# A decoder layer on one core: one cross attention unit's softmax by head on ScalarE, and the values of both segments in one product

## The reference

```python
def attn(x):            # self attention in segments
    qkv = x @ W_qkv     # 16 heads of 16
    q, k, v = ... [:, :, m]            # m: rows of 16 tokens, every second reversed
    # 2 segments of 128 queries; keys and values: every second token (64)
    p = softmax(q_seg @ k_seg.T * 16 ** -0.5)
    return (p @ v_seg)[inverse m] @ W_out

def xattn(x, ctx):      # cross attention, 16 heads of 16, 77 keys
    p = softmax((x @ Wq.T + bq) @ (ctx @ Wk.T + bk).T / 4)
    return (p @ (ctx @ Wv.T + bv)) @ Wo.T + bo

def ffn(x):             # 14 experts of width 512, one for each token
    e = argmax(x @ router_w); w = softmax(x @ router_w)[e]
    return w * (gelu(x @ w1[e] + b1[e]) @ w2[e] + b2[e])

x = layernorm(x + attn(x))
x = layernorm(x + xattn(x, ctx))
x = layernorm(x + ffn(x))
```

## Time and profile before

| | |
|---|---|
| median of 3 runs | 597.56 us (596.89 to 598.15) |
| the profiled execution's own time | 593.98 us |
| its span, first to last instruction | 592.2 us |
| PE, DVE, POOL, ACT busy | 560.5, 463.3, 405.7, 343.1 us |
| mean granted clock of TensorE | 0.977 of full speed |

### The profile page before, as it was taken

How to read it: one execution, slowest core, us unless ns; L and a number is a source line. 1 busy time by engine, 2 the same in 40 slices (tenths; PEclk the granted TensorE clock), 3 DMA queues, 4 the chain that set the end, 5 groups by cost and what they waited for, 6 DMA issues and landing times.

```text
span 592.2 us, 16640 instructions
## 1 busy us (share of the span) xinstructions
PE 560.5 (95%) x5608; PEld 474.9 (80%) x5608; DVE 463.3 (78%) x1071; ACT 343.1 (58%) x842; POOL 405.7 (69%) x554
## 2 busy tenths in 40 slices
PE   7989999999999999999999999799799999999990
PEld 5867788788888888788788778568789999999990
DVE  3778999999999999999999989865455555666661
ACT  2456666666666676676666765546545555555540
POOL 4446675678678677678678766675787677777652
PEclk9899999999999999999999999969989999999996
DMA  7416026126225314313514101114343333333200
GB/s 216 162 24 191 14 52 196 27 68 183 42 60 160 65 40 137 103 51 88 153 34 144 52 10 37 34 39 119 53 112 97 85 87 87 95 92 89 68 16 0
DMA packets 76692, 50.11 MB, mean 85 GB/s; under 512 B 39222, under 2 KB 70970, under 8 KB 76608
## 3 DMA queue, kind: packets, MB, share of 16 engines
q1 hardware_dynamic: 71264, 40.60, 25.5%
q0 software_dynamic: 5344, 8.44, 5.5%
HBM read 40.55 MB, written 10.60 MB: 86 GB/s over the span
## 4 chain that ended last, share of the span: by engine, by line
PE 74%; POOL 9%; issue 7%; DVE 5%; ACT 2%; DMA 1%; POOLq 0%; ACTq 0%; DVEq 0%
PE ps_r L822 15%; PE ps_r L740 13%; PE ps_s L956 11%; PE ps_r L972 10%; PE ps_r L807 5%; PE ps_r L902 5%; PE ps_s L762 4%; PE ps_s L753 3%; POOL token_lists L1579 3%; POOL prob L1498 2%; PE ps_r L795 2%; PE ps_r L879 2%; PE ps_r L897 2%; PE ps_r L904 2%; POOL out L1605 1%
## 5 line engine op out<-in xcount | busy, mean ns | idle before, releaser
L1498 POOL TENSOR_TENSOR prob<-prob,rden 128x616 f32<-128x616 f32 (+1 forms) x96 | 138.4, 1449 | 56.8 <-DVE rden L1173 55.1
L999 ACT COPY probT<-ps_r 128x512 f32<-128x512 f32 x192 | 86.8, 480 | 43.2 <-PE ps_r L740 41.4
L1141 DVE TENSOR_REDUCE mx<-ps_s 128x8 f32<-128x616 f32 (+1 forms) x96 | 88.8, 925 | 19.1 <-PE ps_s L753 12.8
L1019 ACT ACTIVATE prob<-prob 128x616 f32<-128x616 f32 (+1 forms) x96 | 79.4, 833 | 33.8 <-DVE prob L1152 33.6
L1161 DVE TENSOR_REDUCE den<-prob 128x8 f32<-128x616 f32 (+1 forms) x96 | 88.3, 920 | 6.9 <-ACT prob L1019 5.7
L1152 DVE TENSOR_TENSOR prob<-ps_s,mx 128x616 f32<-128x616 f32 (+1 forms) x96 | 89.8, 936 | 4.5 <-PE ps_r L740 3.0
L956 PEld LDWEIGHTS ps_s<-xgT,w1b 128*128 128x128 f32 x720 | 88.0, 193 | 2.5 <-issue 0.3
L740 PE MATMUL ps_r<-ident,prob 128*128 128x128 f32 (+1 forms) x576 | 88.4, 281 | 1.6 <-POOL prob L1498 1.0
L956 PE MATMUL ps_s<-xgT,w1b 128*128 128x128 f32 x720 | 88.6, 276 | 0.2 <-ACT xgT L1107 0.2
L972 PE MATMUL ps_r<-w2s,hT 128*128 x360 | 86.2, 383 | 0.3 <-ACT hT L1119 0.3
L740 PEld LDWEIGHTS ps_r<-ident,prob 128*128 128x128 f32 (+1 forms) x576 | 66.1, 142 | 16.8 <-issue 9.6
(11 more groups left out here) (158 smaller groups left out, 1006.1 us busy)
## 6 DMA issues: line engine op xcount, KB each, us to landing
w1s<-in_w SPq DMA_DIRECT2D x14, 512.0 KB
w2s<-in_w SPq DMA_DIRECT2D x14, 512.0 KB
b2r<-in_b SPq DMA_DIRECT2D x45, 128.0 KB, 3.2
xT<-in_x_cols SPq DMA_DIRECT2D x16, 256.0 KB, 2.9
xres<-in_x SPq DMA_DIRECT2D x16, 256.0 KB
x_rows<-x2s SPq DMA_DIRECT2D x32, 128.0 KB, 1.9
xkT<-in_xk_cols SPq DMA_DIRECT2D x16, 128.0 KB, 2.3
ctxT<-in_ctx_cols SPq DMA_DIRECT2D x16, 77.0 KB, 2.1
```

Source lines behind the costliest of these rows:

```text
L999: nc.scalar.copy(probT[0:rows, par, first:last], src[0:rows, 0:last - first]).then_inc(pT_copied[kind].sem, 1)
L1019: nc.scalar.activation(prob[:, n % 3, 0:width], prob[:, n % 3, 0:width], ACT.Exp, scale=SCALE).then_inc(exp_done[kind].sem, 1)
L1141: nc.vector.tensor_reduce(m, s, axis=AX, op=ALU.max).then_inc(max_done[kind].sem, 1)
L1498: nc.gpsimd.tensor_tensor(p, p, rden[:, par, 0:heads, None].to_broadcast([P, heads, width]), ALU.mult).then_inc(scaled[kind].sem, 1)
```

## The change

1. **Unit 5's softmax (`FUSED = ("x", 3)`).** DVE still takes the maxima, but then makes only `nmx`, the maxima times minus the scale (128x8). ACT reads the scores of each of the eight heads from `ps_s`, with `nmx` as bias, writes the exponentials to `prob` and sums them into `den` with `accum_out`: eight instructions in place of one. DVE's subtraction and its sum are gone for this unit, and the reciprocal waits for ACT.
2. **Who frees `ps_s` behind unit 5.** The next scores wait for `exp_done` (ACT), and so do the first two hidden layers of the expert tiles, which use the same banks.
3. **Values.** `v` is two matmuls of 128x256, keys of both segments on the partitions; ACT places them with four copies of 64x128 (segment by even or odd heads), half of which move them to the other 64 partitions.
4. **Order.** All tables are new, and so is `HELD`.

```diff
+        FUSED = ("x", 3)
+        def wait_read(eng, event, held="", part=""):
+            if event is not None:
+                done = exp_done if event[:2] == FUSED else sub_done
+                wait(eng, done[event[0]], event[2], event[1], held, part)
...
         def pe_scores(pe, n, i):
-            wait_for(pe, sub_done, unit_before(n, i, 1), held="pe_scores.1", part=n)
+            wait_read(pe, unit_before(n, i, 1), held="pe_scores.1", part=n)
...
             elif job == "v":
-                for s in range(NSEG):
-                    for c in range(KC):
-                        heads = wqkv_s[:, c, 2 * D:3 * D].rearrange("p (g o d) -> p g o d", o=2, d=DH)
-                        for o in range(2):
-                            last = nc.tensor.matmul(dst[o * KEYS:(o + 1) * KEYS, s * P:(s + 1) * P],
-                                                    xkT[:, b % 2, c, s, :], heads[:, :, o, :],
-                                                    start=(c == 0), stop=(c == KC - 1))
+                last = project(lambda c: xkT[:, b % 2, c].rearrange("p s k -> p (s k)"), lambda c: wqkv_s[:, c, 2 * D:3 * D])
...
         def pe_hidden(pe, j):
-                wait(pe, sub_done["x"], B - 1)
+                wait(pe, exp_done["x"], B - 1)
...
         def act_exp(act, n, i):
             wait(act, sub_done[kind], b, k, held="act_exp.1", part=n)
+            if (kind, k) == FUSED:
+                third = unit_before(n, i, 3)
+                if third is not None:
+                    wait(act, pT_done[third[0]], third[2], 2 * third[1] + 1, held="act_exp.2", part=n)
+                wait_for(act, rec_done, unit_before(n, i, 2), held="act_exp.3", part=n)
+                for h in range(HH):
+                    last = nc.scalar.activation(prob[:, n % 3, h * K2:(h + 1) * K2],
+                                                ps_s[:, h // RH, h % RH * K2:(h % RH + 1) * K2], ACT.Exp,
+                                                bias=nmx[:, h:h + 1], scale=SCALE, accum_out=den[:, par, h:h + 1])
+                last.then_inc(exp_done[kind].sem, 1)
+                return
...
             elif job == "v":
                 for o in range(2):
-                    rows = slice(o * KEYS, (o + 1) * KEYS)
-                    last = nc.scalar.copy(dst[rows, :, :, o, :],
-                                          src[rows, 0:2 * P].rearrange("p (s g d) -> p s g d", s=NSEG, d=DH))
+                    for n in range(NSEG):
+                        last = nc.scalar.copy(dst[o * KEYS:(o + 1) * KEYS, n, :, o, :],
+                                              from_ps[n * KEYS:(n + 1) * KEYS, :, o, :])
...
         def dve_less_max(dve, n, i):
             wait(dve, max_done[kind], b, k, held="dve_less_max.1", part=n)
+            if (kind, k) == FUSED:
+                wait(dve, exp_done[kind], b - 1, k, held="dve_less_max.3", part=n)
+                nc.vector.tensor_scalar(nmx[:], mx[:, par, 0:HH], -SCALE, None, ALU.mult).then_inc(sub_done[kind].sem, 1)
+                return
...
-        PE_TILES = "y@2 hid@0 rows@-1"
+        PE_TILES = "hid@-2 rows@-3 y@-1"
```

More of the change, by code:

```diff
@@ L38 @@
[L38 to L42, removed]
@@ L46 @@
+    "w1_copy.1:0",
 }
@@ L273, in decoder_layer @@
         exp_done = {u: signal(f"exp_done_{u}", n) for u, n in UN.items()}
-        sum_done = {u: signal(f"sum_done_{u}", n) for u, n in UN.items()}
+        sum_done = {u: signal(f"sum_done_{u}", n if u == "a" else n - 1) for u, n in UN.items()}
         rec_done = {u: signal(f"rec_done_{u}", n) for u, n in UN.items()}
@@ L379, in decoder_layer @@
-            probT50:15 probT51:15 wa:1 rows:0 gate_exp0:13 rt1:14 take_o4:15 take_o5:15 rows:1 gelu:0 rt0:15
-            gelu:1 rt1:15 rows:2 rows:3 wa:2 wa:3 gelu:2 gate_exp0:15 wa:4
+            qx0:13 take_o5:12 gate_exp0:11 probT00:14 probT01:14 take_o0:14 exp2:13 probT10:14 probT11:14
+            exp3:13 k0:15 exp4:13 take_o1:14 q0:15 probT20:13 probT21:13 exp5:13 vx0:14 probT30:13 probT31:13
+            rt0:12 take_o2:13 take_o3:13 probT40:13 kx0:14 probT41:13 probT50:13 x1T0:14 probT51:13 exp0:15
@@ L381, in decoder_layer @@
+            rt0:14 wa:0 take_o5:15 rows:0 rt1:14 wa:1 rows:1 gelu:0 gelu:1 rt0:15 rt1:15 rows:2 rows:3 wa:2 wa:3
+            gate_exp0:15 gelu:2 wa:4
         """
         DVE_FIRST = """
-            max0:0 wr0:0 less_max0:0 wr1:0 max1:0 less_max1:0 sum0:0 reciprocal0:0 sum1:0 reciprocal1:0 max0:1
-            wr2:0 less_max0:1 bo0:0 sum0:1 reciprocal0:1 max1:1 oa0:0 stats10:0 oa1:0 mean10:0 stats11:0
-            mean11:0 ln10:0 ln11:0 less_max1:1 sum1:1 reciprocal1:1 max2:0 less_max2:0 max3:0 less_max3:0 oa0:1
@@ L455, in decoder_layer @@
-            bias_row:1 store_x0:14 bias_row:2 slots:6 slots:7 bias_row:3 bias_row:4 store_x1:14 store_x0:15
-            store_x1:15 slots:8 slots:9 bias_row:5 slots:10
-        """
-        PE_TILES = "y@2 hid@0 rows@-1"
-        ACT_TILES = "wa@-2 rows@-2 gelu@-1"
-        DVE_TILES = "eps@1 bias@0 wd@-4 res@0 stat@0 norm@1 agg@0"
-        POOL_TILES = "gather@-3 pow@3 put@4"
-        SP_TILES = "slots@-2 bias_row@-2"
+            load_xres0:12 place_v0:11 load_e0:13 place_v1:11 place_v2:11 place_v3:11 place_v4:11 load_x0:15
@@ L463, in decoder_layer @@
+            bias_row:1 bias_row:2 bias_row:3 store_x1:13 store_x0:14 store_x1:14 bias_row:4 bias_row:5 slots:7
+            store_x0:15 store_x1:15 slots:8 slots:9 slots:10
+        """
+        PE_TILES = "hid@-2 rows@-3 y@-1"
+        ACT_TILES = "wa@1 gelu@2 rows@0"
+        DVE_TILES = "agg@3 eps@3 bias@2 res@2 wd@-3 stat@2 norm@3"
+        POOL_TILES = "gather@-4 pow@2 put@3"
+        SP_TILES = "slots@3 bias_row@4"
+        FUSED = ("x", 3)
         UNITS = [("a", 0), ("a", 1), ("x", 0), ("x", 1), ("x", 2), ("x", 3)]
@@ L1169, in dve_reciprocal @@
             heads = H if kind == "a" else HH
-            wait(dve, sum_done[kind], b, k, held="dve_reciprocal.1", part=n)
+            if (kind, k) == FUSED:
+                wait(dve, exp_done[kind], b, k, held="dve_reciprocal.1", part=n)
+            else:
+                wait(dve, sum_done[kind], b, k, held="dve_reciprocal.1", part=n)
             wait_for(dve, scaled, unit_before(n, i, 2), held="dve_reciprocal.2", part=n)
```

209 lines of the change are left out of this document (107 added, 102 removed).

## The result

The changed kernel takes 619.14 us (median; three of its runs lie between 617.85 and 619.83, the fourth was disturbed and is not in the ratio) against 597.53 us for the kernel before: ratio 1.0352, 95% interval [1.0316, 1.0388]. Forecast were 611.0 us, range 595 to 624. The profiled execution took 617.85 us, its span is 616.1 us. The experiments ran on four chips. On two of them the kernel before takes 595 to 596 us; on the other two it takes 635 to 638 us at a mean granted clock of TensorE of 0.93 to 0.95 (0.97 to 0.98 on the first two). So total times are compared by ratio on one chip, and pairs of batches in stretches at the upper level of the clock (2.4 GHz).

A forecast was written before the change was run, and what follows sets the result against it. The prediction took TensorE as the bound, full in the attention part. New waits +17.5 us, value product -2.6 and VectorE relief -1.5 gave +13.4: 607.4 us for the profiled execution, 611.0 us as the median, range 595 to 624.

The forecast's parts named there:

- TensorE's new wait at unit 0's scores, on ScalarE's last head: Between batches, scores wait until ScalarE has read unit 5's PSUM banks: 1.8 us in even batches, 0.9 in odd.
- E: Length of unit 5's eight ScalarE activations with sums: taken as 2.63 us, between 1.86 and 5.2 us.
- The fourth rival: Unit 5's activations: each sum costs an instruction of its own, E = 3.9 us, total 628 us; chance 0.08.
- The pair of batches: Steady attention part: a pair of batches takes 48.8 us instead of 46.4.
- The value product: Value projection on TensorE: 0.87 us instead of 1.03, saving 0.16 us 16 times, 2.6 us in all.
- The four copies at nothing: ScalarE's copies of the values: 0.34 us more per batch, costed at nothing since values are used half a batch later.
- VectorE, 22.6 us less: Unit 5's subtraction becomes a small product and its sum goes: 1.41 us less VectorE work per batch.
- half of TensorE's waiting near 380 us: Two score jobs there wait 2.98 us for VectorE; its relief was taken to save 1.5 us, ends 0 and 3.0.
- The order at nothing, 2 us either way: Start of the program: two batches' keys and queries projected before the first scores, some weights fetched later; costed at nothing.
- The second rival: Whole kernel: VectorE sets the pace, ScalarE has room and the activations overlap (E = 1.86), 594.3 us, faster; chance 0.20.
- The third: TensorE's clock: the new idle time in even batches sends it to its lower level, 15.6 us more, 626.6 us; chance 0.07.
- The fifth: The new waits fall where TensorE would have waited anyhow: -2.6 to 0 us, total 595 to 598 us; chance 0.05.

The follow-up runs named there:

- e3: Kernel before with only unit 5's eight activations added, old order and old value product kept: ratio 1.0129 to the kernel before.
- e6: Changed kernel with unit 5's eight activations handing over no sums (its divisions use unit 3's): 611.71 us against 596.45 for the kernel before.
- e12: The changed kernel itself, run again on another chip: ratio 1.0382 to the kernel before.
- e1: Kernel before with only the value product changed (one product for both segments, four ScalarE copies instead of two): 638.86 us against 638.37, ratio 1.0012.
- e8: The same kernel as e1, run once more: 640.28 us against 634.91 for the kernel before, ratio 1.0065.
- e10: Changed kernel (new order and value product) with unit 5's softmax as in the kernel before: ratio 1.0330 to the kernel before.

## Why the prediction was right, and where its sizes were off

- **TensorE's new wait at unit 0's scores, on ScalarE's last head**: right. Predicted 1.8 and 0.9 us; measured 1.39 (with 0.33 more at the transpose that waits for the rank's bank, so 1.72 in an even batch) and 0.79. TensorE's busy share between 100 and 340 us is 95%, under the 96% that was named. e3 shows it from the eight alone, e6 that it follows the group's length one for one.
- **E**: taken as 2.63 us, measured 2.58. The reason was half right: eight activations with sums don't overlap freely, but none waits until the sum before it is out: the second starts at 247.16, the first one's read ends at 247.26. They start 0.30 us apart, with a read of 222 ns between them that overlaps both neighbours; without it 0.22 apart (e6, 1.84 for eight), the 1.86 of the lower bound. An estimate from the Trainium skill ("ScalarE: Activation LUTs", What ACT_TABLE_LOAD costs), 2.10 with no price for the sum's output, lies between the two. The fourth rival had the instruction right (a read of its own) and its price wrong: it is not added in full, 0.09 us a head comes out.
- **The pair of batches**: predicted 48.8 us, measured 48.84, in e12 48.81. So close an agreement is luck: the waits that were forecast come to 2.51 us and not to 2.75, and a wait of 0.30 us that was not forecast, at cross attention's output projection, makes up for it.
- **The value product**: its length, 0.87, was right; its worth wasn't. With its copies it is worth nothing (e1, e8). For the waits at the scores this did no harm in the sum, because the same 0.16 us had been added to each of them: when the banks are released sets the time there, not when TensorE arrives.
- **The four copies at nothing**: a step that failed. The prediction asked when the values are used; what counts is what stands behind their copies in ScalarE's queue. There stand the `oTx` copies, for which TensorE's next projection waits: 0.30 us in a pair, in the changed kernel as in e8.
- **VectorE, 22.6 us less**: measured 21.1. That it would buy half of TensorE's waiting near 380 us, 1.5 us, was wrong. The stretch 380 to 420 us has less of TensorE than before (34.33 against 35.70) and the same clock of 0.87, and the end of the program takes 2.7 us more in the profiled execution, 0.9 in e12. Part of the difference between these two is the clock: near 450 us the profiled execution is at the lower level for 6.8 us, e12 and the kernel before for 3.4.
- **The order at nothing, 2 us either way**: the largest miss of the sum, 4.5 us at the start (3.3 in e12). The order's own part wasn't separated from the start's own spread. In the steady part the new order costs 1.9 us a pair with the old softmax (e10).
- **The rest**: the pairs from 2 to 14 cost 15.9 us where the terms make 14.6; 2.2 of it is one pair (51.0 us, in e12 49.7) with a wait of 2.2 us at a transpose in batch 6 that the profile puts down mostly to "issue"; its cause stays open. And the median of the changed kernel lies 1.3 us above its profiled execution, not 3.6.

So 611.0 + 4.5 (start) + 4.6 (3.4 at the end and from batch 14 on, where the terms make -1.2) + 1.3 (pairs) - 2.3 = 619.1.

The second rival (VectorE sets the pace) fell: VectorE is lighter, and the kernel slower. Yet it had a point that the forecast missed: TensorE's work was not all that set the pace, or the shorter value product would have paid. What stood just ahead of TensorE, where a releaser can be seen, was ScalarE's copies (of q and of `oTx`), not VectorE. The third (the clock) fell in the result: both kernels' steady pairs are at the upper level there. The fifth fell.

## What to carry to other kernels

Before an operation that reads a PSUM bank is exchanged for a longer one on another engine, write down who needs the bank next and how long the reader will hold it: here 0.8 us on VectorE became 2.6 us on ScalarE, in a place where the next product stood ready. A TensorE that shows no idle time may still be just in time at some places; before counting a shorter job as a gain, look how long before its next jobs the copies that they wait for end, and try the shorter job with no other engine's work changed. Work moved to an engine with free time is not free either, if a copy that TensorE needs stands behind it in the queue. And an order that was searched for one balance of engines is not neutral for another: try the operation in the old order and the new order without the operation, since neither alone need show the sum.

## What the runs showed of the hardware

An activation with an accumulated sum is two instructions in the trace, the second an ACTIVATION_READ_ACCUMULATOR of 222 ns (x128), most of it beside its neighbours.

On the two chips where the kernel before takes 635 to 638 us, TensorE's results reach ScalarE late some microseconds before the recorded granted clock falls. In e1, in an even batch, ScalarE and TensorE:

```profile
250.42 1.07 ACT L1034 COPY vA<-ps_r 64x128 f32<-64x128 f32 x4
254.12 0.27 ACT L1006 COPY oTx<-ps_r 128x128 f32<-128x128 f32 x1 [2.63 <-remote]
255.66 0.27 ACT L1006 COPY oTx<-ps_r 128x128 f32<-128x128 f32 x1 [1.28 <-remote]
```

```profile
250.15 1.36 PE L807 MATMUL ps_r<-probT,vX 128*32 128x128 f32 x32
251.44 1.07 PE L740 MATMUL ps_r<-ident,prob 128*128 128x128 f32 x5
256.07 1.24 PE L896 MATMUL ps_r<-wo_s,oTx 128*128 128x272 f32 x3 [3.56 <-ACT oTx L1006]
```

ScalarE copies what the products at 250.15 wrote, 2.6 us after their modelled end at 251.5; the next copy is late by another 1.3 us, and at 256.6 the recorded clock goes to its lower level of 1.2 GHz for 6.8 us. TensorE stands 2.5 to 3.7 us at this place in five even batches of e1 and of e8. The likeliest reading is that the products themselves ran slowly; the records don't show their ends, so this was not shown. If it is right, "remote" and a wait of TensorE for ScalarE can be TensorE's own slowness.
